# A decoder's linear attention set closer together inside a SwiGLU mixture, and eight maxima of the next cross attention placed there instead of five

## What is computed

```python
# L1 feed-forward: SwiGLU mixture, 8 experts and a shared one (D = 256), top 2
g = silu(einsum('th,ehd->etd', xt, Wg)); u = einsum('th,ehd->etd', xt, Wu)
out_all = einsum('etd,edh->eth', g * u, Wd)      # weighted by the gates, summed into x
# L2 attention ("linear attention" here): sequence 4 (the batches), 256 x 16 heads of 8
qkv = (einsum('sbe,fe->sbf', x, in_proj_weight) + in_proj_bias) * gamma
scores = einsum('bsd,btd->bst', q / sqrt(8), k)  # s, t = 0..3, causal over the batches
out = softmax(scores) @ v; out = ((out * alpha) @ Wout.T + bout) * lgamma
# L2 cross attention, 16 heads of 8
ctx = softmax(einsum('bhqd,bhkd->bhqk', q, k) / sqrt(8)) @ v; x = x + ctx @ w_concat.T
```

## The kernel before

| step | w before | w after |
|---|---|---|
| turn_norm (L2a) | 1, 2 | 1, 2 |
| l2_project, l2_take | 3, 5 | 3, 4 |
| l2_weights | 4, 6 | 4, 5 |
| exponentials, both | 7 | 6 |
| l2_values | 8, 10 | 7, 8 |
| l2_close | 9, 11 | 8, 9 |
| turn_close | 11, 13 | 9, 10 |
| project_out (PE), l2_add (DVE) | 12, 14 | 10, 11 |
| normalised X2 (DVE) | 13, 15 | 11, 12 |
| turn_norm X2 | 15, 17 | 12, 13 |
| slots of X2 | 22 to 26 (5) | 19 to 26 (8) |

## Time and profile before

### The profile page before, as it was taken

How to read it: one execution, slowest core, us unless ns; L and a number is a source line. 1 busy time by engine, 2 the same in 40 slices (tenths; PEclk the granted TensorE clock), 3 DMA queues, 4 the chain that set the end, 5 groups by cost and what they waited for, 6 DMA issues and landing times.

```text
span 1244.7 us, 19906 instructions
## 1 busy us (share of the span) xinstructions
PE 1014.1 (81%) x7630; PEld 548.4 (44%) x7649; DVE 811.4 (65%) x2024; ACT 611.7 (49%) x1018; POOL 241.2 (19%) x305
## 2 busy tenths in 40 slices
PE   5777679998999965667576889999758878769999
PEld 4233223333677652334353233466412333336757
DVE  7786867741324477888867884477688787665412
ACT  2556346666334427777753777423115556423342
POOL 2833300000000223674542000000222000000000
PEclk9789879999899995677767999999858889889999
DMA  8333040000000310238012500800100300100000
GB/s 302 95 78 79 30 176 2 2 2 1 1 1 1 90 46 1 82 123 149 6 38 71 176 2 2 141 1 1 52 14 28 115 1 2 34 1 1 1 9 9
DMA packets 34785, 61.23 MB, mean 49 GB/s; under 512 B 4771, under 2 KB 25076, under 8 KB 33092
## 3 DMA queue, kind: packets, MB, share of 16 engines
q1 hardware_dynamic: 33828, 58.64, 16.7%
q10 hardware_dynamic: 864, 1.33, 0.3%
HBM read 42.91 MB, written 16.65 MB: 48 GB/s over the span
## 4 chain that ended last, share of the span: by engine, by line
PE 57%; DVE 30%; ACT 5%; issue 4%; DMA 1%; POOL 1%; SPq 0%; DVEq 0%; ACTq 0%; POOLq 0%
PE ps_e L865 9%; PE ps_s L875 9%; PE ps_v L668 6%; DVE mx L1841 6%; PE ps_e L604 5%; PE ps_s L625 3%; PE ps_e L602 3%; DVE ps_s L1837 2%; PE ps_e L969 2%; ACT work L1382 2%; DVE mx L1831 2%; PE ps_s L956 2%; DVE work L2320 2%; DVE work L2322 2%; DVE xn L1797 2%
## 5 line engine op out<-in xcount | busy, mean ns | idle before, releaser
L1382 ACT ACTIVATE work<-ps_e 128x512 f32<-128x512 f32 x448 | 250.7, 598 | 140.1 <-PE ps_e L604 135.3
L2595 POOL TENSOR_TENSOR rstd<-rstd,halves 128x2 f32<-128x2 f32 x52 | 36.6, 704 | 694.9 <-DVE rstd L1784 694.7
L1841 DVE TENSOR_REDUCE mx<-ps_s 128x2 f32<-128x1024 f32 x128 | 153.9, 1222 | 25.6 <-PE ps_s L625 24.3
L625 PE MATMUL ps_s<-ctx_stack,q_stack 49*128 49x512 bf16 (+1 forms) x384 | 127.5, 452 | 45.1 <-DVE mx L1841 32.2
L604 PE MATMUL ps_e<-q_stack,ctx_stack 52*128 52x256 bf16 (+1 forms) x768 | 149.2, 291 | 17.2 <-issue 6.4
L1484 ACT ACTIVATE work<-ps_s,keep 128x512 f32<-128x512 f32 x136 | 93.0, 687 | 137.0 <-PE ps_s L875 134.0
L668 PE MATMUL ps_v<-work,vaug 128*32 128x256 f32 x1536 | 127.8, 408 | 4.5 <-ACT work L1370 4.3
L865 PEld LDWEIGHTS ps_e<-ffn_w,work 128*128 128x128 f32 x960 | 118.2, 196 | 21.1 <-issue 19.9
L865 PE MATMUL ps_e<-ffn_w,work 128*128 128x128 f32 x960 | 120.0, 280 | 0.8 <-DVE x L2031 0.8
L875 PE MATMUL ps_s<-xnT,ffn_w 128*128 128x512 f32 x240 | 115.6, 605 | 4.2 <-ACT work L1484 4.2
L2041 DVE SCALAR_TENSOR_TENSOR x<-ps_e,gates,x 128x128 f32<-128x128 f32 x128 | 38.9, 346 | 120.7 <-PE ps_e L865 117.7
(11 more groups left out here) (379 smaller groups left out, 1803.8 us busy)
## 6 DMA issues: line engine op xcount, KB each, us to landing
q_stack<-q_scr SPq DMA_DIRECT2D x32, 192.0 KB
ffn_w<-in_L0f_w SPq DMA_DIRECT2D x1, 4608.0 KB, 14.5
ffn_w<-in_L1f_w SPq DMA_DIRECT2D x1, 3456.0 KB, 13.1
q_scr<-parts SPq DMA_DIRECT2D x16, 192.0 KB, 2.1
c_scr<-ffn_w SPq DMA_DIRECT2D x12, 256.0 KB, 7.7
kx_scr<-ffn_w SPq DMA_DIRECT2D x12, 256.0 KB, 3.3
ctx_stack<-kx_scr SPq DMA_DIRECT2D x2, 1536.0 KB
ctx_stack<-c_scr SPq DMA_DIRECT2D x2, 1536.0 KB
```

The costliest lines, as they stand in the source:

```text
L625: return pe.matmul(ps_s[i][:, parity, :], q_stack[p0:p0 + n_rows, b, pair, part * P:(part + 1) * P], ctx_stack[p0:p0 + n_rows, pair, b * S ...
L1382: act.activation(pt[:, parity, :, :].rearrange("p k q -> p (k q)"), bank[f"e{parity}"], ACT.Exp).then_inc(exped, 1)
L1841: m = dve.tensor_reduce(mx[:, b, :, pair, part], ps_s[i][:], AX, ALU.max, negate=True)
```

## The change

The steps of batches 0 and 1 move to the windows of the table, on PE, ACT and DVE alike. `EARLY_X2` becomes 8, so slots 0 to 7 run in w = 19 to 26 and the loop starts at slot 8. Batch 2's steps follow it, from slot 9 instead of 6; batch 3's start at slot 21 instead of 20. POOL's and SP's programs are as before, and no instruction is added or removed.

```diff
-EARLY_X2 = 5
+EARLY_X2 = 8
+L2_SLOT = {2: EARLY_X2 + 1, 3: 21}
...
# PE
-            if w in (3, 5):
-                l2_project((w - 3) // 2, window_tile)
-            if w in (11, 13):
-                turn_close("L2a", (w - 11) // 2)
-            if w in (12, 14):
-                project_out("L2a", (w - 12) // 2, kp("L2a_outT"), window_tile)
-            if w in (15, 17):
-                turn_norm(X2, (w - 15) // 2)
+            if w in (3, 4):
+                l2_project(w - 3, window_tile)
+            if w in (9, 10):
+                turn_close("L2a", w - 9)
+            if w in (10, 11):
+                project_out("L2a", w - 10, kp("L2a_outT"), window_tile)
+            if w in (12, 13):
+                turn_norm(X2, w - 12)
...
-            for b, at in ((2, t - 6), (3, t - 20)):
+            for b, at in ((b, t - L2_SLOT[b]) for b in (2, 3)):
...
# ACT
-            if w == 7:
+            if w == 6:
                 l2_exp_of(0)
                 l2_exp_of(1)
-            if w in (11, 13):
-                turned_close("L2a", (w - 11) // 2)
-            if w in (15, 17):
-                turned_norm(X2, (w - 15) // 2, qT, scale=RSQRT8)
+            if w in (9, 10):
+                turned_close("L2a", w - 9)
+            if w in (12, 13):
+                turned_norm(X2, w - 12, qT, scale=RSQRT8)
...
# DVE
-            if w in (3, 5):
-                l2_take((w - 3) // 2, 1)
-            if w in (4, 6):
-                l2_weights((w - 4) // 2)
-            if w in (8, 10):
-                l2_values((w - 8) // 2)
-            if w in (9, 11):
-                l2_close((w - 9) // 2)
-            if w in (12, 14):
-                l2_add((w - 12) // 2, 1)
-            if w in (13, 15):
-                normalised(X2, (w - 13) // 2)
+            if w in (3, 4):
+                l2_take(w - 3, 1)
+            if w in (4, 5):
+                l2_weights(w - 4)
+            if w in (7, 8):
+                l2_values(w - 7)
+            if w in (8, 9):
+                l2_close(w - 8)
+            if w in (10, 11):
+                l2_add(w - 10, 1)
+            if w in (11, 12):
+                normalised(X2, w - 11)
```

## The result

The changed kernel takes 1260.92 us (median of 11 runs, 1259.28 to 1273.57) against 1251.53 before in the same runs. The ratio is 1.0104 with a 95% interval of 1.0078 to 1.0130: 13 us slower (9.8 to 16.3); the two medians lie 9.4 apart. Forecast were +11.2 us and 1262.3, with the chance of "slower by over 1%" put at 0.36. The centre of the interval lies just over that line, the difference of the medians under it, so which side it is on isn't settled.

A forecast was written before the change was run, and what follows sets the result against it. PE was taken to bound the mixture's second half and DVE's maxima the stretch after it. The terms 6.3 + 4.2 - 3.5 + 3.2 + 1.0 gave +11.2 us, 1262.3 on the median of 1251.1; range 1248 to 1272.

The forecast's parts named there:

- Part 1: Squeezed chain, windows w=3 to 13: PE stands 3.1, 1.4 and 2.8 us, so unit 15 is reached 6.3 us later.
- The fill of slot 0: Query fill before slot 0: lands at about 886.1, slot 0 comes at 890.2, so the earlier 1.01 us wait goes.
- Part 2: Eight slots in the windows, unit 15 to the mixture's last gated sum: 20.4 us against 17.2, up to +5.1; +4.2 taken.
- Parts 3 and 4: Behind the mixture: three maxima fewer, -3.5 us; DVE standing for POOL's root at batch 3's normalisation, +3.2 us.
- Part 5: PE's clock around the stands and down steps: none to two falls, 0 to +3.6 us, +1.0 taken.
- rival (a): Clock falls in both chain gaps and over down step 16: +15 to +17 us, 1267; chance 0.33.
- Rival (b): DVE's work is the only currency; three maxima fill its idle time from 880 to 898: -3.5 us, 1247.6; chance 0.12.
- Rival (c): Batch 0's close is early, so the first two stands do not come, but POOL loops stay: +6 us, 1257; chance 0.13.

The follow-up runs named there:

- slots_only: The kernel before with eight slots in the windows and batch 3 at slot 21, the chain in its old windows: ratio to before 1.0053.
- chain_only: The changed kernel's squeezed chain windows, but with five slots and batch 3 at slot 20 as in the kernel before: ratio to before 1.0069.
- silu_roots: Changed kernel with POOL computing the next batch's root before splitting queries, and ACT's exponentials at w=7 instead of 6: ratio to before 1.0019.

## Why the prediction was right

The sign and the steps came out, and the size within what the runs can tell; one term, the clock, was mis-sized. Point by point, against the profiled execution:

- **Part 1, stands.** Predicted 3.1, 1.4 and 2.8, measured 2.88, 1.05 and 2.61. The walk through DVE's queue used row durations where the next start comes up to 0.1 earlier; with start-to-start times, the lower bound named, it would have been nearer. Net of the 0.83 of before that is 5.7, where 6.3 was said. The two causes named, the Silu behind the exponentials and the root behind the split, were each taken away by an edit of its own and took 1.36 and 2.61 with them.
- **The fill of slot 0.** Its wait went, as said. That it was not worth having is shown by slots_only.
- **Part 2.** From unit 15 to the last gated sum 22.8 (888.42 to 911.20) against 17.2: +5.5, where +4.2 was taken and +5.1 was the upper bound. Both down steps 16 and 17 ran at the lower level (3.78 and 3.63): the case priced at 1.9 more, and counted half. The other 0.4 over the bound is the slots at the lower level, which start 1.93 apart (905.06 to 906.99) where 1.7 was taken.
- **Parts 3 and 4.** Together -0.3 predicted; B is 78.2 in both kernels. The stand for batch 3 was 4.33, predicted 4.2. Taking it away by POOL's order gave 3.0 in B; by moving batch 3 two slots, 1.4. So the +3.2 is borne out by one run and not by the other, and the -3.5 has no run of its own.
- **Part 5, the clock.** This is the term that was mis-sized: +1.0 was taken with 0 to +3.6 as bounds. Unit 15 began 9.4 later against the first projection, the stands make 5.7 of that, and nearly all of the other 3.7 is matmuls at the lower level behind the first and third stand (3.3 by their starts), among them an up half's last products 866.43 to 868.07, 1.64 instead of 0.86; the down step 879.77 to 882.84, 3.07 instead of 1.79. The granted clock over 845 to 880 is 0.95 where it was 1.00, and 0.72 over 866 to 872 and over 880 to 886. The step of the prediction that failed is this choice of the low end: I leaned on the dense rows of before, in which PE had not once stood for 2.6 us.
- **The sum.** +11.2 predicted, +14.9 in A and B of this execution, +13 by the ratio. Against the 14.9 the terms were off by +2.7 (part 5), +1.3 (part 2), +0.3 (parts 3 and 4) and -0.6 (part 1), so the clock makes nearly all of it. By its mechanism, then, what happened is rival (a), which had the falls behind the stands and over down step 16: with its 3.6 and 5.1 in the forecast's own sum, the sum is 14.7. Its 15 to 17 came from upper bounds of parts 1 and 4 that were not reached. That the forecast of 1262.3 lies 1.4 us from the median is in part luck. Rival (b) is refuted by chain_only: the squeeze, with three stands in PE's queue, costs 8.6 us with DVE's work unchanged. Rival (c) did not come: the first stands were there.

The Trainium skill's drain of about 1.38 us behind a table load ("ScalarE: Activation LUTs", "What ACT_TABLE_LOAD costs") does not show here either. In silu_roots the load starts at 857.53 and the exponentials at 858.83, 1.30 later. Going by the row was right.

## What to carry to other kernels

Where one engine is dense and takes its work in order, count a chain's hand-overs against the dense engine's work between the two windows: a chain may be drawn together only until its slowest hand-over equals that work, and past that the dense engine pays each difference in full, and may pay again in matmuls at the lower clock. Look for the link in the chain that waits only because of its place in a third engine's queue: here new orders on POOL and ACT alone gave back most of the loss (12.6 of the 14.9 in A and B), though they didn't make the changed kernel faster than the one before. And work that fills a gap can be free once per gap (A was 41.9 with one slot a gap and 41.7 with none); a second piece in the same gap, on the same single buffer, waits for the first, here 1.3 to 2.0 us each, with matmuls at the lower clock behind it. Such a gain in one stretch must still be looked for in the whole: here B gave it back.

## What the runs showed that I had not expected

The last 270 us of the program are the same instructions in all these kernels, yet took 268.7 to 276.1 us in their profiled executions. The stretch of before from 976, and the one of the changed kernel from the matching addition:

```profile
976.00:1245.00 269.00, 227.33 (x1484) 139.59 (x1483) 149.28 (x442) 110.51 (x211) 14.12 (x20) 0.92 0.02 7
```
```profile
989.40:1265.00 275.60, 233.51 (x1484) 142.64 (x1483) 149.57 (x443) 110.73 (x211) 14.13 (x20) 0.89 0.03 12
```

The same 1484 matmuls, 6.2 us more of PE and 0.89 instead of 0.92 of the clock, while DVE's and ACT's times are equal to 0.3. The whole span differs between executions of one kernel too: those of the changed kernel had spans of 1257.8 us at a granted clock of 0.878, of 1265.1 at 0.869 and of 1272.1 at 0.863. An edit of a few us can therefore be judged in a single profile only by the stretches it touches; the whole span of one execution would have said +20.8 here.
